# Layer 3 self-attention on one Trainium2 core: half of the penalties' products on GpSimd instead of VectorE

## The chip, the cores and the metric

One Trainium2 chip, one of its cores, one launch. The time is device microseconds of that core for the whole kernel, a twelve-part decoder (four layers of self-attention, cross-attention and feed-forward). Engines are named as the profile names them: PE is TensorE's matmul stream and PEld its weight loads, DVE is VectorE, ACT is ScalarE, POOL is GpSimd, SP is SyncE, which issues the loads.

## The reference

Tokens are x[16,128,256], seen as (2, 512, 256) or (4, 512, 256) by some layers and as 16 blocks of 128 here. The part that the change touches is layer 3's self-attention:

```python
g = sigmoid(x @ Wg + bg)
res = (1 - Z_I) * max(1 - Z_I - Z_J, 0) + Z_I * min(1 - Z_I + Z_J, 1)
penalties = res * clip(base ** (1 - g) + 2 - abs_ij, 1e-32, 1)
scores = q @ k.T / sqrt(16) + log(max(penalties, 1e-32))    # 16 heads of 16
ctx = softmax(scores) @ v
x = layernorm(x + ctx)
```

The kernel does not add the logarithm ahead of the exponential. It multiplies exp(scores) by the penalties, one 128x128 table per block, the same for all heads; the sum of each row comes out of the product with V, which has columns of ones.

## The kernel before, in words

`attention16` serves several attentions. `l3_attentions` calls it with two parts in one pipeline: 16 "own" blocks (the self-attention, with penalties) and then 16 "crossed" blocks (the cross-attention, without). A block is 128 tokens with 16 heads, handled in two halves of 8 heads; a half is one 128x1024 float32 tile. Its stages are spread over turns: `for n in TURNS` on each engine writes out by hand what that engine does in turn n, in order, and engines meet at counted semaphores (`since(engine, event, b)` waits until event has counted block b). Nothing else orders the work.

In turn n, of own blocks:
- PE (L2402): scores of block n, first half, interleaved with the transposed scores of block n-1, half 1 (`scores(n, 0)`, L2301 and L2306); `attend(n-2)` (L2336), half 1 and then half 0 of the probabilities `Pr` times V, each after `w_done[half]`; queries of block n+1; the transposes of a finished block (L2384); then `before_second(n)`, which waits for `mx_ready[0]`, and `scores(n, 1)`; after it the transposes of the output (L2343), the keys of n+1 (L2256), the transposes of the maxima (L2368) and the values of n+1 (L2267).
- ACT (L2506): the exponentials of block n-1, half 1 after `scores(n, 0)` and half 0 after `scores(n, 1)` (L2447, they count `e_done[half]`); between them copies out of PSUM, and the keys' placing (L2478).
- DVE (L2607): `maximum(n, 0)` (L2547); `spread(n-3)`, the moments of a row (L2595 to L2599); **`weigh(n-1, 1)`** (L2560); `maximum(n, 1)` (L2547); `scaled(n-3)` (L2605); `put_maxima(n)` (L2554); `weigh(n-1, 0)` (L2560); `normalise(n-2)` (L2579, L2584).
- POOL (L2227): `move_v(n)` (L2196); `root(n-3)` (L2221); `own_query(n+1)`, four instructions (L2210); `store(n-3)` (L2225), after `scaled(n-3)`; `own_residual(n-2)` (L2217), after `normalise(n-2)`.

`weigh(b, half)` multiplies the 128x1024 tile of probabilities in place by the penalties' 128x128 table, read again for each of the 8 heads:

```python
dve.tensor_tensor(Pr[b % 2][half][:].rearrange("p j c n -> p (j c) n"),
                  Pr[b % 2][half][:].rearrange("p j c n -> p (j c) n"),
                  part(b).penalty[:, b, :].unsqueeze(1).to_broadcast([P, NH * SLOTS16, P]),
                  ALU.mult).then_inc(w_done[half], 1)
```

Turn n = 1 is the first with a `weigh` (block 0) and turn 16 the last (block 15). Two buffers of `Pr` are used in turn (`b % 2`); the exponential of block b waits for `attend(b-2)`. Other lines that the prediction uses: L1878, a POOL product `tensor_tensor(k2, k2, table, mult)` of a 128x1024 tile in place with a 128-wide table, in another stage; L4400, L4503 and L4504, POOL and DVE operations on 128x512 tiles in the stage that makes the penalties. The stage after the attention asks for its first data at L3190 once the attention has ended.

Of the kernel before, what the change touches and what calls it, by code (L numbers as in the profile page):

```python
# [8 lines left out]
ALU = mybir.AluOpType  # L9
# [7 lines left out]
P = 128  # L17
# [19 lines left out]
NH = P // ROWS // 2  # L37
# [2022 lines left out]
def attention16(core, a, name, parts, after=()):  # L2060


    with Stage(core, name) as s:
        SCALE = float(DH) ** -0.5
        LIFT = 60.0
        SLOTS16 = KD * PAIR
# [23 lines left out]
        Pr = [[s.sb(f"Pr{w}_{i}", [P, NH, SLOTS16, P]) for i in range(2)] for w in range(2)]  # L2090
# [30 lines left out]
        e_done = [s.sem(f"e_done{i}") for i in range(2)]  # L2121
        w_done = [s.sem(f"w_done{i}") for i in range(2)]
# [13 lines left out]
        def live(b):  # L2136

            return 0 <= b < LAST

        def own(b):  # L2140

            return live(b) and part(b).own

        def crossed(b):

            return live(b) and not part(b).own

        def part(b):

            return parts[b // NB]  # L2150

        def block_of(b):

            return b % NB

        def since(eng, event, b):

            if b >= 0:
                eng.wait_ge(event, min(b, LAST - 1) + 1)
# [6 lines left out]
        @block.sync  # L2166
        def _(sp):
            for later in after:
                later.request(sp, a)

        @block.gpsimd
        def _(pool):
            pool.memset(mx[:], 0.0).then_inc(m_cleared, 1)
            if any(p.penalty is not None for p in parts):
                pool.memset(lift[:], LIFT).then_inc(lift_ready, 1)
            for t in V:
                pool.memset(t[:], 1.0).then_inc(v_cleared, 1)
            for p in parts:
                p.early.wait(pool)
                if p.moved:  # L2180
                    pool.wait_ge(biases_ready, 1)
            pool.wait_ge(v_cleared, len(V))

            def sum_q(b):
                since(pool, q_turned, b)
                since(pool, q_stored, b - 1)
                pool.tensor_tensor(q32[:], rq[0][:], rq[1][:], ALU.add).then_inc(q_summed, 1)

            def move_v(b):
                since(pool, o_ready, b - len(V))  # L2190
                out = V[b % len(V)][:, :, 0:DH]
                if part(b).values is not None:
                    ins = pool.tensor_copy(out, part(b).values[:, block_of(b), :].rearrange("p (h d) -> p h d", d=DH))
                else:
                    since(pool, v_copied, b)
                    ins = pool.tensor_tensor(out, v32[:].rearrange("p (h d) -> p h d", d=DH),  # L2196
                                             part(b).early.bvt[:].rearrange("p (h d) -> p h d", d=DH), ALU.add)
                ins.then_inc(v_stored, 1)

            def residual(b):  # L2200
                since(pool, r_ready, b - 1)
                since(pool, x_stored, b - NB)
                x = core.X[:, block_of(b), :]
                pool.tensor_tensor(xres[:], x, part(b).early.bot[:], ALU.add).then_inc(xres_ready, 1)

            def own_query(b):
                since(pool, q_copied, b)
                since(pool, t_ready[0], b - 4)
                for c in range(SLOTS16):
                    ins = pool.tensor_scalar(qx[b % 4][:, c, :], q32[:, c % KD, :], own_rows[:, c // KD:c // KD + 1],  # L2210
                                             bqm[:, c:c + 1], ALU.mult, ALU.add)
                ins.then_inc(q_stored, 1)

            def own_residual(b):
                since(pool, normal, b)
                since(pool, xn_ready, b - 1)
                pool.tensor_tensor(r[:], O[:], core.X[:, block_of(b), :], ALU.add).then_inc(r_ready, 1)  # L2217

            def root(b):
                since(pool, ve_ready, b)  # L2220
                pool.tensor_tensor(rstd[:], ve[:], core.mhalf[:], ALU.pow).then_inc(rstd_ready, 1)  # L2221

            def store(b):
                since(pool, xn_ready, b)
                pool.tensor_copy(core.X[:, block_of(b), :], xn[:]).then_inc(x_stored, 1)  # L2225

            for n in TURNS:  # L2227
                if crossed(n - 3):
                    residual(n - 3)
                if live(n):  # L2230
                    move_v(n)
                if own(n - 3):
                    root(n - 3)
                if own(n + 1):
                    own_query(n + 1)
                if own(n - 3):
                    store(n - 3)
                if crossed(n - 4):
                    root(n - 4)
                if rope and live(n + 1):  # L2240
                    sum_q(n + 1)
                if crossed(n - 4):
                    store(n - 4)
                if own(n - 2):
                    own_residual(n - 2)
# [285 lines left out]
        def _(dve):  # L2531
# [11 lines left out]
            def maximum(b, half):  # L2543
                since(dve, s_ready[half], b)
                since(dve, m_ready, b - 1)
                out = mx[:].rearrange("p t (e c) -> p e t c", c=DH)[:, NH * PAIR * half:NH * PAIR * (half + 1), :, 0]
                dve.tensor_reduce(out, pR[:].rearrange("p j (i t) n -> p (j i) t n", i=PAIR), AX.X, ALU.max  # L2547
                                  ).then_inc(mx_ready[half], 1)
# [9 lines left out]
            def weigh(b, half):  # L2558
                since(dve, e_done[half], b)
# [5 lines that stand above are left out]
            def rotate(b):  # L2565
                since(dve, q_ready, b)
                since(dve, q_summed, b - 1)
                for out, table in ((rq[0], early.cosT), (rq[2], early.sin_partner)):
                    for t in range(KD):
                        ins = dve.scalar_tensor_tensor(out=out[:, t, :], in0=pq[:, t, :], scalar=early.bqc[:, t:t + 1],  # L2570
                                                       in1=table[:], op0=ALU.add, op1=ALU.mult)
                ins.then_inc(q_placed, 1)
                dve.wait_ge(q_placed, b + 1)
                dve.stream_shuffle(out=rq[1][:].rearrange("p k n -> p (k n)"), in_=rq[2][:].rearrange("p k n -> p (k n)"),
                                   mask=partners()).then_inc(q_turned, 1)
# [17 lines left out]
            def spread(b):  # L2593
                dve.wait_ge(r_ready, b + 1)
                dve.bn_stats(stats[:], r[:]).then_inc(stats_ready, 1)  # L2595
                dve.wait_ge(stats_ready, b + 1)
                dve.bn_aggr(mv[:], stats[:]).then_inc(mv_ready, 1)
                dve.wait_ge(mv_ready, b + 1)
                dve.tensor_scalar(ve[:], mv[:, 1:2], LN_EPS, None, ALU.add).then_inc(ve_ready, 1)  # L2599
# [7 lines left out]
            for n in TURNS:  # L2607
                if live(n):
                    maximum(n, 0)
                if own(n - 3):  # L2610
                    spread(n - 3)
                if crossed(n - 4):
                    spread(n - 4)
                if own(n - 1):
                    weigh(n - 1, 1)
                if rope and live(n + 1):
                    rotate(n + 1)
                if live(n):
                    maximum(n, 1)
                if own(n - 3):  # L2620
                    scaled(n - 3)
                if crossed(n - 4):
                    scaled(n - 4)
                if live(n):
                    put_maxima(n)
                if own(n - 1):
                    weigh(n - 1, 0)
                if live(n - 2):
                    normalise(n - 2)
                if crossed(n - 3):  # L2630
                    residual(n - 3)
# [2061 lines left out]
```

## Time and profile before

| | us |
|---|---|
| median of 3 runs | 2595.38 (2594.41 to 2601.98) |
| the profiled execution | 2594.83 |
| its span | 2593.0 |
| PE busy | 2283.1 (88%) |
| DVE busy | 1314.9 (51%) |
| POOL busy | 709.2 (27%) |

The span is the time from the first to the last recorded instruction; the profiled execution's own time has 1.8 us around it. The rows below are quoted from the page and from answers of the trace: "x4" is a count of merged instructions, and "[0.64 <-PE a_pR L2301]" says that the engine sat idle for 0.64 us before the instruction and which work ended that. Where several instructions are merged, the duration is that of the whole group. Instructions on one engine can overlap a little at their ends, so the distance between two starts can be slightly less than a duration.

### The profile page before, as it was taken

How to read it: one execution, taken by the hardware profiler on the slowest of the kernel's cores; microseconds unless marked ns; L12 is line 12 of the kernel's file. 1: busy time of each engine (PE TensorE's matmuls, PEld its weight loads, DVE VectorE, ACT ScalarE, POOL GpSimd, SP SyncE). 2: the span in 40 equal slices, each digit the busy share in tenths (PEclk: the TensorE clock that was granted, in tenths of full speed). 3: DMA queues.
4: the chain of work that ended last, by engine and by line, in shares of the span. 5: the costliest groups of instructions: out<-in, count | busy, mean ns of one | idle time of the engine just before them, and what ended most of it. 6: DMA issues, size and time to landing. Idle time of an engine off the chain costs nothing. (4 is left out here: it accounts for less than half of the span.)

```text
span 2593.0 us, 48661 instructions
## 1 busy us (share of the span) xinstructions
PE 2283.1 (88%) x18360; PEld 1789.3 (69%) x18369; DVE 1314.9 (51%) x2768; ACT 906.4 (35%) x1591; POOL 709.2 (27%) x1096
## 2 busy tenths in 40 slices
PE   8869999787989899999979988976977989599992
PEld 4647777453567565899968866645865778399992
DVE  4466666598668421111157754553137887511114
ACT  2233333484356301111122224521225667122223
POOL 1722222235223100122212221211325633133332
PEclk9889999898989999999999998987988999799996
DMA  7500000100020100788710003012530000399994
GB/s 281 190 1 1 0 0 1 26 1 1 1 92 2 52 0 1 269 315 316 259 51 0 0 3 95 2 52 83 165 84 5 2 2 3 116 322 327 325 325 139
DMA packets 162728, 253.57 MB, mean 98 GB/s; under 512 B 17296, under 2 KB 123536, under 8 KB 162320
## 3 DMA queue, kind: packets, MB, share of 16 engines
q1 hardware_dynamic: 153360, 230.42, 25.8%
q0 software_dynamic: 9216, 21.06, 3.0%
q8 instruction: 103, 1.69, 0.3%
q14 instruction: 49, 0.40, 0.0%
HBM read 219.79 MB, written 31.13 MB: 97 GB/s over the span
## 5 line engine op out<-in xcount | busy, mean ns | idle before, releaser
L3516 PE MATMUL te_pU<-te_xsT,te_wu 128*128 128x128 f32 x1952 | 233.5, 276 | 1.5 <-DVE te_xsT L3609 1.5
L3516 PEld LDWEIGHTS te_pU<-te_xsT,te_wu 128*128 128x128 f32 x1952 | 231.1, 193 | 5.2 <-issue 2.1
L3537 PE MATMUL te_pY<-te_wd,te_hT 128*128 128x256 f32 x976 | 220.8, 379 | 0.0
L3537 PEld LDWEIGHTS te_pY<-te_wd,te_hT 128*128 128x128 f32 x976 | 180.7, 190 | 22.1
L1230 PE MATMUL x_pB<-early,x_xlT 128*128 128x384 f32 x376 | 133.4, 499 | 1.7 <-ACT x_xlT L1362 1.7
L3566 ACT ACTIVATE te_hT<-te_pU 128x512 f32<-128x512 f32 x78 | 46.6, 597 | 234.9 <-PE te_pU L3516 234.9
L2547 DVE TENSOR_REDUCE x_mx<-x_pR 128x8 f32<-128x1024 f32 x64 | 78.3, 1223 | 78.0 <-PE x_pR L2301 78.0
L3590 DVE COPY te_ys<-te_pY 128x256 f32<-128x256 f32 x61 | 25.9, 425 | 162.8 <-PE te_pY L3537 162.8
L3585 DVE TENSOR_TENSOR te_hT<-te_pU,te_sg 128x512 f32<-128x512 f32 x44 | 30.4, 692 | 147.5 <-ACT te_sg L3564 147.5
L3564 ACT ACTIVATE te_sg<-te_pG 128x512 f32<-128x512 f32 x44 | 26.3, 597 | 210.2 <-PE te_pG L3516 210.2
L1230 PEld LDWEIGHTS x_pB<-early,x_xlT 128*128 128x128 f32 x376 | 68.8, 193 | 43.1 <-issue 4.3
L2547 DVE TENSOR_REDUCE a_mx<-a_pR 128x8 f32<-128x1024 f32 x64 | 78.3, 1224 | 34.2 <-PE a_pR L2301 34.1
L2449 ACT ACTIVATE x_Pr<-x_pT 128x1024 f32<-128x1024 f32 x64 | 65.6, 1025 | 79.8 <-PE x_pT L2306 79.8
L3587 DVE COPY te_xsT<-te_pT 128x256 f32<-128x256 f32 x61 | 25.7, 421 | 130.6 <-PE te_pT L3510 130.6
L2301 PE MATMUL a_pR<-a_kx,a_qx 32*128 32x128 f32 x1024 | 74.6, 282 | 17.1 <-ACT a_kx L2478 6.3
L3478 POOL COPY te_home<-moe_home 128x1 uint32 (+1 forms) x61 | 11.1, 181 | 285.0 <-DVE te_ys L3590 285.0
L2301 PEld LDWEIGHTS a_pR<-a_kx,a_qx 32*128 32x128 f32 x1024 | 63.4, 186 | 33.1 <-issue 20.0
L3516 PE MATMUL te_pG<-te_xsT,te_wg 128*128 128x128 f32 x704 | 85.8, 275 | 0.0
L2301 PEld LDWEIGHTS x_pR<-x_kx,x_qx 32*128 32x128 f32 x1024 | 66.5, 196 | 25.0 <-issue 21.7
L2301 PE MATMUL x_pR<-x_kx,x_qx 32*128 32x128 f32 x1024 | 79.0, 294 | 4.3 <-DVE x_qx L2554 3.7
L3516 PEld LDWEIGHTS te_pG<-te_xsT,te_wg 128*128 128x128 f32 x704 | 82.1, 192 | 0.0
L3468 POOL DMA_INDIRECT te_xs<-xs_slots,te_token x65 | 64.8, 997 | 51.9 <-POOL te_token L3465 51.9
(669 smaller groups left out, 5627.1 us busy)
## 6 DMA issues: line engine op xcount, KB each, us to landing
te_wu<-in_L_ffn_w_upT SPq DMA_DIRECT2D x39, 1024.0 KB, 5.9
te_wd<-in_L_ffn_w_downT SPq DMA_DIRECT2D x39, 1024.0 KB, 5.8
te_wu<-in_L_ffn_up SPq DMA_DIRECT2D x22, 1024.0 KB, 4.9
te_wg<-in_L_ffn_gate SPq DMA_DIRECT2D x22, 1024.0 KB, 6.9
te_wd<-in_L_ffn_down SPq DMA_DIRECT2D x22, 1024.0 KB, 7.6
moe_first<-in_L_ffn_W SPq DMA_DIRECT2D x8, 1024.0 KB, 8.5
xs_slots<-zeros SPq DMA_DIRECT2D x1, 5120.0 KB, 15.6
ys_slots<-zeros SPq DMA_DIRECT2D x1, 5120.0 KB, 28.9
```

Of the source, the lines that this page charges most:

```text
L1230: ins = pe.matmul(to[:, n, 0:HALF], xlT[t][:, src + k, :], w[:, k, bass.ts(n, HALF)], start=(k == 0), stop=(k == KD - 1))
L2301: return pe.matmul(pR[:, j, c, :], qx[b % 4][g, c, :], kx[b % 4][g, c, :], start=mask is None, stop=mask is None or c == SLOTS16 - 1)
L2449: ins = act.activation(Pr[b % 2][half][:], pT[:], ACT.Exp, scale=SCALE)
L2547: dve.tensor_reduce(out, pR[:].rearrange("p j (i t) n -> p (j i) t n", i=PAIR), AX.X, ALU.max).then_inc(mx_ready[half], 1)
L3468: pool.indirect_dma_start(xs[u][:], None, core.XS, bass.IndirectOffsetOnAxis(token[u][:, 0:1], 0)).then_inc(x_loaded[u], 16)
L3516: ins = pe.matmul(out[g][:, m, :], w[:, k, bass.ts(PER * g + m, P)], xsT[:, k, :], start=(k == 0), stop=(k == KD - 1))
L3537: ins = pe.matmul(pY[u][:, 0, :], hT[:, k, :], wd[u][:, k, :], start=(k == 0), stop=(k == KH - 1))
L3564: act.activation(sg[g][:], pG[g][:], act_fn).then_inc(g_done, 1)
L3566: act.activation(hT[:, PER * g:PER * (g + 1), :], pU[g][:], act_fn).then_inc(h_done, 1)
L3585: dve.tensor_tensor(hT[:, PER * g:PER * (g + 1), :], pU[g][:], sg[g][:], ALU.mult).then_inc(h_done, 1)
L3587: dve.tensor_copy(xsT[:], pT[:, 0:KD, :]).then_inc(xT_stored, 1)
L3590: dve.tensor_copy(ys[u][:], pY[u][:, 0, :]).then_inc(y_used, 1)
```

## The change

`weigh(n-1, 1)` is taken out of DVE's order of turn n, where it stood between `spread` and `maximum(n, 1)`. POOL gets a `weigh` of its own, for half 1 alone, placed behind `store(n-3)` and ahead of `own_residual(n-2)`. The operands, the event waited for (`e_done[1]`) and the event counted (`w_done[1]`) are the same; half 0 stays on DVE.

```diff
--- before.py
+++ after.py
@@ -2216,6 +2216,12 @@
                 since(pool, xn_ready, b - 1)
                 pool.tensor_tensor(r[:], O[:], core.X[:, block_of(b), :], ALU.add).then_inc(r_ready, 1)
 
+            def weigh(b):
+                since(pool, e_done[1], b)
+                pr = Pr[b % 2][1][:].rearrange("p j c n -> p (j c) n")
+                pool.tensor_tensor(pr, pr, part(b).penalty[:, b, :].unsqueeze(1).to_broadcast([P, NH * SLOTS16, P]),
+                                   ALU.mult).then_inc(w_done[1], 1)
+
             def root(b):
                 since(pool, ve_ready, b)
                 pool.tensor_tensor(rstd[:], ve[:], core.mhalf[:], ALU.pow).then_inc(rstd_ready, 1)
@@ -2235,6 +2241,8 @@
                     own_query(n + 1)
                 if own(n - 3):
                     store(n - 3)
+                if own(n - 1):
+                    weigh(n - 1)
                 if crossed(n - 4):
                     root(n - 4)
                 if rope and live(n + 1):
@@ -2611,8 +2619,6 @@
                     spread(n - 3)
                 if crossed(n - 4):
                     spread(n - 4)
-                if own(n - 1):
-                    weigh(n - 1, 1)
                 if rope and live(n + 1):
                     rotate(n + 1)
                 if live(n):
```

## Rows read from the trace of the kernel before

**Rows 1.** Page: the span and the busy time of each engine.

```profile
span 2593.0 us, 48661 instructions
...
PE 2283.1 (88%) x18360; PEld 1789.3 (69%) x18369; DVE 1314.9 (51%) x2768; ACT 906.4 (35%) x1591; POOL 709.2 (27%) x1096
```

**Rows 2.** Windows, turns 3-13, 14-16: length, PE, PEld, DVE, ACT, POOL, PEclk.

```profile
2000.22:2089.32 89.10, 80.98 (x1365) 68.06 (x1366) 78.96 (x133) 57.53 (x110) 55.46 (x90) 1.00 0.01 2
2089.32:2111.22 21.90, 17.74 (x341) 14.44 (x342) 20.03 (x35) 14.76 (x27) 9.73 (x16) 1.00 0.01 1
```

**Rows 3.** Timeline of DVE, turns 8 and 9: start, duration, instruction, [idle before].

```profile
2040.72 1.23 DVE L2547 TENSOR_REDUCE a_mx<-a_pR 128x8 f32<-128x1024 f32 x1 [0.64 <-PE a_pR L2301]
...
2041.86 0.50 DVE L2605 TENSOR_SCALAR a_xn<-a_r,a_mv,a_rstd 128x256 f32<-128x256 f32 x1
...
2042.54 0.88 DVE L2554 SCALAR_TENSOR_TENSOR a_qx<-a_pX,place,a_qx 128x256 f32<-128x256 f32 x2 [0.17 <-PE a_pX L2368]
...
2043.33 1.22 DVE L2560 TENSOR_TENSOR a_Pr<-a_Pr,early 128x1024 f32<-128x1024 f32 x1
...
2045.09 1.22 DVE L2547 TENSOR_REDUCE a_mx<-a_pR 128x8 f32<-128x1024 f32 x1
...
2046.96 1.22 DVE L2560 TENSOR_TENSOR a_Pr<-a_Pr,early 128x1024 f32<-128x1024 f32 x1
...
2048.82 1.23 DVE L2547 TENSOR_REDUCE a_mx<-a_pR 128x8 f32<-128x1024 f32 x1 [0.64 <-PE a_pR L2301]
```

**Rows 4.** Timeline of PE in turns 8 and 9.

```profile
2043.79 0.34 PE L2301 MATMUL a_pR<-a_kx,a_qx 32*128 32x128 f32 x1 [0.42 <-ACT a_kx L2478]
...
2045.28 1.08 PE L2336 MATMUL a_pO<-a_Pr,a_V 128*32 128x128 f32 x32 [0.31 <-issue]
...
2047.28 0.38 PE L2384 MATMUL a_pk<-ident,a_xn 128*128 128x128 f32 x2
...
2047.60 0.37 PE L2301 MATMUL a_pR<-a_kx,a_qx 32*128 32x128 f32 x1
```

**Rows 5.** Timeline of POOL in turns 8 and 9.

```profile
2040.48 1.73 POOL L2210 TENSOR_SCALAR a_qx<-a_q,own_rows,a_bqm 128x128 f32<-128x128 f32 x4
...
2042.43 0.40 POOL L2225 COPY X<-a_xn 128x256 f32<-128x256 f32 x1 [0.21 <-DVE a_xn L2605]
...
2045.26 0.73 POOL L2217 TENSOR_TENSOR a_r<-a_O,X 128x256 f32<-128x256 f32 x1 [2.44 <-DVE a_O L2584]
...
2047.12 1.46 POOL L2221 TENSOR_TENSOR a_rstd<-a_ve,mhalf 128x1 f32<-128x1 f32 x1 [0.44 <-DVE a_ve L2599]
```

**Rows 6.** Timeline of DVE: second maxima of turns 3, 14, 15 and 17.

```profile
2000.22 1.23 DVE L2547 TENSOR_REDUCE a_mx<-a_pR 128x8 f32<-128x1024 f32 x1 [0.42 <-PE a_pR L2301]
...
2089.32 1.23 DVE L2547 TENSOR_REDUCE a_mx<-a_pR 128x8 f32<-128x1024 f32 x1 [0.64 <-PE a_pR L2301]
...
2096.70 1.22 DVE L2547 TENSOR_REDUCE a_mx<-a_pR 128x8 f32<-128x1024 f32 x1
...
2111.22 1.23 DVE L2547 TENSOR_REDUCE a_mx<-a_pR 128x8 f32<-128x1024 f32 x1 [0.83 <-PE a_pR L2301]
```

**Rows 7.** One line's instructions on POOL: products and roots, min/median/max ns.

```profile
L1878 POOL TENSOR_TENSOR a_turned<-a_turned,early x4: 2347/2794/2797, 597.8 to 637.4; 128x1024 f32<-128x1024 f32 x4
...
L2221 POOL TENSOR_TENSOR a_rstd<-a_ve,mhalf x32: 548/550/1491, 1998.7 to 2221.9; 128x1 f32<-128x1 f32 x32
```

**Rows 8.** Timeline of POOL and DVE where both work on 128x512 tiles.

```profile
1953.73 1.54 POOL L4400 TENSOR_TENSOR ao_high<-ao_oz,ao_zj 128x512 f32<-128x512 f32 x1 [2.79 <-ACT ao_oz L4456]
...
1953.68 0.69 DVE L4503 TENSOR_TENSOR ao_low<-ao_oz,ao_zj 128x512 f32<-128x512 f32 x1 [0.74 <-ACT ao_oz L4456]
...
1954.41 1.41 DVE L4504 SCALAR_TENSOR_TENSOR ao_low<-ao_low,ao_oz 128x512 f32<-128x512 f32 x1
```

**Rows 9.** Timeline of POOL and DVE beside POOL's 128x1024 products.

```profile
597.75 2.35 POOL L1878 TENSOR_TENSOR a_turned<-a_turned,early 128x1024 f32<-128x1024 f32 x1
...
605.59 2.80 POOL L1878 TENSOR_TENSOR a_turned<-a_turned,early 128x1024 f32<-128x1024 f32 x1
...
597.81 14.66 DVE L2009 SCALAR_TENSOR_TENSOR a_cv<-a_xi,early,a_cv 128x512 f32<-128x512 f32 x6 [2.90 <-ACT a_cv L1956]
```

**Rows 10.** Timeline of SP's queue after the attention.

```profile
2224.08 0.38 SPq L3190 DMA_DIRECT2D xs_slots<-X  x1
```

## The prediction

> **What bounds the kernel now.** I read the page's first part, then the windows over the stage, then the timelines of one turn engine by engine, and last the durations of single lines. The page says that PE is busy for 88% of the span and POOL for 27% [rows 1]. That is an average over many stages and says nothing of this one. In the turns that the change touches, the windows show PE busy 80.98 of 89.10 us, DVE 78.96, POOL 55.46 [rows 2]: PE and DVE are both near full, and the granted clock is 1.00, so TensorE has its full 2.4 GHz. One turn is the distance between two second maxima, (2089.32 - 2000.22)/11 = 8.10 us [rows 6].
>
> DVE in one turn [rows 3]: the second maxima at 2040.72 came 0.64 us after DVE had run out of work, because PE's scores were late. So the product that the change removes (2046.96, the half 1 product of block 8) stands ahead of a wait for PE, 0.64 us long. What opens PE's second scores at 2047.60 is PE's own row of work: `attend` at 2045.28, queries, then the transposes at 2047.28 with 0.38 us [rows 4]. The first maxima, which they also wait for, end at 2045.09 + 1.22 = 2046.31 [rows 3], 1.29 us early. PE's first scores wait 0.42 us for ACT's keys [rows 4], again not for DVE. So in turns 3 to 13 PE with ACT sets the pace, and DVE follows closely. In turns 14 and 15 it is DVE: no idle time stands before 2096.70, and that turn took 2096.70 - 2089.32 = 7.38 us [rows 6].
>
> **What is removed.** One DVE product per turn, 1.22 us, some 1.14 us from start to next start, 16 times. In turns 3 to 13 that only lengthens DVE's idle 0.64 us: worth nothing. Where DVE sets the pace it is worth at most 1.14 us per turn, if nothing else is late. It also ends a collision: POOL's root takes 1.46 us at 2047.12, beside this product [rows 5], and 0.55 us in the median of the stage [rows 7]. That is off the path, since POOL then idles 2.44 us ahead of L2217 [rows 5].
>
> **What is added.** One product on POOL per turn. L1878 is its near twin (in place, both inputs in SBUF, 128x1024, a repeated table): 2.35 us at the least and 2.80 at the most [rows 7]. I take 2.35, the instruction at 597.75 that began with DVE idle [rows 9]; 2.80 is the upper end, beside DVE work. POOL has room: 55.46 us busy in 11 turns is 5.04 per turn [rows 2], minus 0.91 for the root, plus 2.35, makes 6.5 of 8.10. The hole is exactly where the product is put, between the store's end at 2042.43 + 0.40 = 2042.83 and L2217 at 2045.26 [rows 5]. 2042.83 + 2.35 = 2045.18 is 0.10 us ahead of `attend` at 2045.28 [rows 4]. By durations alone the change would cost nothing.
>
> **The collision.** But DVE's other product, half 0 of the same block, starts at 2043.33 [rows 3], inside that interval, and both instructions read two tiles of SBUF. What then happens is shown elsewhere in the trace. L4504 on DVE takes 1.41 us when it starts at 1954.41, while POOL's L4400 runs from 1953.73 to 1955.27; the like operation before it, L4503, took 0.69 [rows 8]. It ended at 1955.82, 0.55 us after POOL's: it had waited for POOL, with only 0.69 - 0.55 = 0.14 us of its own done meanwhile. Six DVE operations of that size took 14.66 us, 2.44 each, beside POOL's products of 2.35 to 2.80 [rows 9]: about one DVE operation passed per POOL operation. The root's 1.46 us is the same with DVE first. So whoever starts first holds the other up, and here POOL starts first, by 2043.33 - 2042.83 = 0.50 us.
>
> The Trainium skill, "SBUF — State Buffer", section "Who interferes with whom", says the same of a VectorE instruction with two SBUF inputs against a GpSimd instruction that reads SBUF, and speaks of an exclusive lock held for the whole instruction. Taken to the letter (1.22 us after POOL's end in place of 1.08) it would add 0.14 us per turn, about 2 us in all; the rows show the 0.14 overlapped, and the sum goes by them.
>
> **The sum for one turn**, in us after the start of the second maxima (2040.72 is 0):
> - POOL's `own_query` ends later than now: POOL's L2217 and all behind it move with DVE's late normalise, the root gives back 0.91, and about 0.2 is left. The store then ends at 2.11 + 0.2 = 2.3.
> - POOL's product runs from 2.3 to 4.65. DVE's wants to start at 2.61 and is held; it ends at 4.65 + 1.22 - 0.14 = 5.73, instead of 3.83.
> - `attend` takes half 1 first, which is ready at 4.65, 0.1 late. Half 0 starts now at 2045.28 + 0.5 - 2040.72 = 5.06 and would start at about 5.8: 0.74 late. PE has no slack behind it (queries, transposes, second scores), so the turn grows by 0.74.
> - By DVE: from the product to the first maxima it is 2045.09 - 2043.33 = 1.76, so these end at 5.73 - 1.22 + 1.76 + 1.22 = 7.49; they are needed at 6.88 (2047.60). That gives 0.61, beside and not on top of the other.
>
> I take 0.7 us per turn. A turn of 8.8 us holds it steadily, as each delay is repeated and not piled up.
>
> **The stage.** Turns 3 to 13, 11 x 0.7 = 7.7 us. Turns 14 and 15, paced by DVE: the blocked product adds about 1.7 us and the removed one gives back 1.14, so 0.6 and 0.5. Turn 16: DVE is 1.64 late, the next second maxima have 0.83 of idle time before them [rows 6], so 0.8. Turns 1 and 2, while the pipeline fills, nothing: there POOL and DVE idle more than a product's length. Sum 9.6 us. Nothing later takes it up: the next stage asks for its rows only at 2224.08 [rows 10], after the attention, so the rest moves as a block. Against the profiled execution's 2594.83 us this is 2604.4; the median of the runs, 2595.38, stands 0.55 above that execution, within its scatter, and I keep 2604.4.
>
> **Rivals.** A measurement of this kernel can tell about 0.3%, 7.8 us, from no change. The forecast stands only just beyond that.
> - **Forecast, POOL first, +9.6 us**, 0.62. With the uncertain terms: if the product takes 2.80, +0.45 per turn and 14 turns, +6; if DVE is held shorter (a POOL instruction's last part free of reads; in rows 9, 0.69 + 2.35 = 3.04 was done in 2.8), 0.3 less per turn, -4. So +5.5 to +16.
> - **No hold-up that reaches the path, 0 us**, 2594.8, 0.17. Half 0 is ready at 3.83 now and needed at 5.06; if DVE's product is held for less than that 1.23 us, PE and the maxima take it up. For it: this slack, and POOL's hole, which fits to 0.1 us. Against it: rows 8 and 9 show the hold.
> - **DVE first**, slower, +17 us, 2612, 0.12. If POOL's store slips past 2.61, DVE's product runs first and POOL's ends at 3.83 + 2.0 = 5.8; `attend` takes half 1 first, and waits from 4.56 to 5.85, 1.3 per turn, 13 turns. Against it: the margin is 0.3 to 0.5 us, and the delay it makes gives POOL time to be early in the next turn.
> - **Faster**, the other side: if PE's pace in turns 14 to 16 follows DVE alone and the two products miss each other there and before, 3 x 1.14 = 3.4 us at most, 2591.4. It would need POOL's product to be over by 2.61, 0.3 us after it starts, or DVE to read past it, and would still be within 0.3%. More than that would need PE's wait of 0.42 us to be for DVE, and the row names ACT. 0.09 with unknown gains, 0.04 of them beyond 0.3%.
>
> The forecast's own spread crosses the bound of 7.8 us, so slower is 0.60, the same 0.36, faster 0.04. The range, 2596 to 2611, takes in both ends of the hold-up, most of the longer product, and leaves out the extreme cases on either side.
>
> **What would show it.** In the profile after: L2560 falls from 32 to 16 instructions and each shows about 3.1 us (from 2.61 to 5.73) instead of 1.22; POOL's product shows 2.35 us, right behind L2225; the root falls to 0.55; the second maxima are 8.8 us apart; PE is idle some 0.7 us inside `attend`, waiting for DVE. Wrong would be: L2560 still at 1.22 with turns of 8.1 (no hold-up); POOL's product at 3 us or more and `attend` late at its first half (DVE first); or turns longer than 9.2 us.

## The result and the profile after

| | before | after |
|---|---|---|
| median | 2594.89 us (4 runs) | 2633.09 us (2631.60 to 2635.69, 4 runs) |
| ratio | | 1.0144, 95% interval 1.0132 to 1.0157 |
| the profiled execution | 2594.83 us | 2635.69 us |

The change made the kernel 38 us slower. The direction was forecast; the size, +9.6 us, was four times too small, and the range ended at 2611. The page of the changed kernel begins so; DVE and POOL are busy about as long as before in all, beside [rows 1]:

```profile
span 2633.9 us, 48661 instructions
...
PE 2302.9 (87%) x18360; PEld 1804.8 (69%) x18369; DVE 1318.8 (50%) x2752; ACT 906.2 (34%) x1591; POOL 732.8 (28%) x1112
```

Windows over turns 3 to 13 and 14 to 16 of the changed kernel, the same turns as in [rows 2]. The columns are length, busy time (instructions) of PE, PEld, DVE, ACT and POOL, granted clock, DMA:

```profile
2007.87:2121.49 113.62, 88.08 (x1365) 74.20 (x1366) 82.89 (x122) 57.46 (x110) 70.84 (x101) 0.92 0.01 2
2121.49:2150.82 29.33, 20.70 (x341) 16.88 (x342) 22.57 (x34) 15.45 (x27) 14.22 (x18) 0.88 0.01 1
```

Turns 3 to 13 took 113.62 us instead of 89.10, turns 14 to 16 29.33 instead of 21.90. That is 32.0 of the 40.9 us by which the two spans differ. The granted clock fell from 1.00 to 0.92 and 0.88, which no row of before had announced. Another 0.8 us is in the first turns of the stage; 6.9 us had passed before the stage began and 1.2 us came behind it, in parts that the change does not touch.

The two products, summed up over the stage (count, then min/median/max ns), and then DVE around one turn, with the second maxima at 2059.25 and 2070.26. They answer to [rows 7] and [rows 3]:

```profile
L2222 POOL TENSOR_TENSOR a_Pr<-a_Pr,early x16: 2352/2358/2365, 1992.7 to 2142.5; 128x1024 f32<-128x1024 f32 x16
...
L2568 DVE TENSOR_TENSOR a_Pr<-a_Pr,early x16: 1576/2800/2814, 1994.5 to 2143.1; 128x1024 f32<-128x1024 f32 x16
```

```profile
2051.38 0.88 DVE L2562 SCALAR_TENSOR_TENSOR a_qx<-a_pX,place,a_qx 128x256 f32<-128x256 f32 x2 [0.28 <-PE a_pX L2376]
...
2052.17 2.81 DVE L2568 TENSOR_TENSOR a_Pr<-a_Pr,early 128x1024 f32<-128x1024 f32 x1
...
2055.18 0.42 DVE L2592 TENSOR_TENSOR a_O<-a_pO,a_R 128x256 f32<-128x256 f32 x1
...
2055.52 1.22 DVE L2555 TENSOR_REDUCE a_mx<-a_pR 128x8 f32<-128x1024 f32 x1
...
2059.25 1.23 DVE L2555 TENSOR_REDUCE a_mx<-a_pR 128x8 f32<-128x1024 f32 x1 [1.77 <-PE a_pR L2309]
...
2070.26 1.23 DVE L2555 TENSOR_REDUCE a_mx<-a_pR 128x8 f32<-128x1024 f32 x1 [3.11 <-PE a_pR L2309]
```

POOL's product takes 2.36 us every time, as its near twin did at its shortest (2.35). DVE's takes 2.80 us instead of 1.22: issued at 2052.17, it ends at 2054.98. POOL in the same turn, the answer to [rows 5]:

```profile
2051.17 0.40 POOL L2231 COPY X<-a_xn 128x256 f32<-128x256 f32 x1 [0.74 <-DVE a_xn L2613]
...
2051.53 2.36 POOL L2222 TENSOR_TENSOR a_Pr<-a_Pr,early 128x1024 f32<-128x1024 f32 x1
...
2055.68 0.73 POOL L2217 TENSOR_TENSOR a_r<-a_O,X 128x256 f32<-128x256 f32 x1 [1.79 <-DVE a_O L2592]
...
2057.55 0.55 POOL L2227 TENSOR_TENSOR a_rstd<-a_ve,mhalf 128x1 f32<-128x1 f32 x1 [0.46 <-DVE a_ve L2607]
```

POOL's product ends at 2053.89 and DVE's 1.09 us later, where the prediction had 1.08. The root is at 0.55 us. So both products and the root behave as forecast; only the start of POOL's product is 0.3 us earlier, which makes the hold-up shorter. The Trainium skill, "SBUF — State Buffer", section "Who interferes with whom", says that the instruction that comes second is blocked until the first has finished; the trace agrees, except that some 0.13 us of the 1.22 is done meanwhile.

What was not forecast is on PE. Its timeline, the attend and the queries of two turns, the answer to [rows 4]:

```profile
2055.70 1.08 PE L2344 MATMUL a_pO<-a_Pr,a_V 128*32 128x128 f32 x32 [1.90 <-DVE a_O L2592]
...
2056.72 1.16 PE L2264 MATMUL a_pq<-XT,early 128*128 128x128 f32 x8
...
2065.39 1.93 PE L2344 MATMUL a_pO<-a_Pr,a_V 128*32 128x128 f32 x32 [1.90 <-DVE a_O L2592]
...
2067.25 1.64 PE L2264 MATMUL a_pq<-XT,early 128*128 128x128 f32 x8
```

`attend` starts at 2055.70, after the end of DVE's `normalise` at 2055.18 + 0.42 = 2055.60, not after the product with which it works. Its wait is 1.90 us in both turns, where [rows 4] show 0.31. In the second of them the same 32 matmuls take 1.93 us instead of 1.08 and the queries 1.64 instead of 1.16. Windows of 10 us around these and two further turns have the granted clock as the third number from the end of a row:

```profile
2050.00:2060.00 10.00, 7.68 (x129) 6.50 (x129) 7.85 (x12) 5.54 (x11) 6.73 (x11) 1.00 0.01 2
2060.00:2070.00 10.00, 7.68 (x119) 6.44 (x117) 6.78 (x11) 4.51 (x10) 5.40 (x8) 0.83 0.01 2
2090.00:2100.00 10.00, 7.67 (x102) 6.43 (x104) 7.17 (x11) 4.78 (x10) 5.24 (x8) 0.83 0.01 2
2100.00:2110.00 10.00, 7.68 (x144) 6.50 (x141) 7.54 (x11) 5.34 (x11) 6.74 (x10) 1.00 0.01 2
```

The turn ending at 2059.25 took 9.69 us and the one ending at 2070.26 11.01. In turns 3 to 13 there are six of 9.68 or 9.69 us and five of 11.00 to 11.22.

### The profile page after: what moved, and what is told of

It reads as the page before. It is cut to its first block and busy times, and to the rows that moved or that the text cites. A ratio compares the mean times of both kernels' runs of the same rounds, so it can differ in the third digit from the quotient of the medians.

```text
span 2633.9 us, 48661 instructions
## 1 busy us (share of the span) xinstructions
PE 2302.9 (87%) x18360; PEld 1804.8 (69%) x18369; DVE 1318.8 (50%) x2752; ACT 906.2 (34%) x1591; POOL 732.8 (28%) x1112
```

## Theories

Theory A: three things in a row. POOL's product, placed in POOL's hole, holds up DVE's product of the other half. DVE's `normalise` stands behind that product, and `attend(b)` on PE begins with a wait for `normalise(b-1)`, so the whole delay reaches PE. And PE's wait of 1.90 us costs granted clock in about every second turn. Its rivals: B, that 2.36 us of POOL per turn is too much or too late wherever it stands; that the long turns come from the order of the waits and not from the clock; and that the changed program is slower elsewhere too. The expectations below were written before each run.

## The experiments

**DVE's order.** In the changed kernel, `normalise(n-2)` goes ahead of `weigh(n-1, 0)`:

```diff
-                if own(n - 1):
-                    weigh(n - 1, 0)
                 if live(n - 2):
                     normalise(n - 2)
+                if own(n - 1):
+                    weigh(n - 1, 0)
```

> The changed kernel with normalise(n-2) ahead of weigh(n-1, 0) on DVE. Theory A (attend waits for normalise, which stands behind DVE's held product, and PE's wait of 1.90 us also costs granted clock): the held product stays (2.8 us beside POOL's 2.36) but attend's first half no longer waits for it, only its second half does; PE's longest wait falls from 1.9 us to under 1 us, turns fall from 9.69/11.1 us to about 8.8 us, and the kernel to about 2606 us (the 0.7 us per turn of the prediction). Theory B (POOL's product is itself too late for attend, or something outside the order of these two costs the time): turns stay above 9.5 us and the time above 2625 us.

Measured 2600.97 us (2599.76 to 2609.78, 10 runs), ratio to before 1.0025 (1.0011 to 1.0039). DVE, PE and POOL in one turn:

```profile
2053.37 0.42 DVE L2592 TENSOR_TENSOR a_O<-a_pO,a_R 128x256 f32<-128x256 f32 x1
...
2053.71 2.18 DVE L2568 TENSOR_TENSOR a_Pr<-a_Pr,early 128x1024 f32<-128x1024 f32 x1
...
2059.05 1.23 DVE L2555 TENSOR_REDUCE a_mx<-a_pR 128x8 f32<-128x1024 f32 x1 [1.29 <-PE a_pR L2309]
...
2054.96 0.65 PE L2344 MATMUL a_pO<-a_Pr,a_V 128*32 128x128 f32 x16 [0.24 <-POOL a_Pr L2222]
...
2055.95 0.64 PE L2344 MATMUL a_pO<-a_Pr,a_V 128*32 128x128 f32 x16 [0.35 <-DVE a_Pr L2568]
...
2052.44 2.37 POOL L2222 TENSOR_TENSOR a_Pr<-a_Pr,early 128x1024 f32<-128x1024 f32 x1
```

The hold-up is still there: DVE's product takes 2.18 us beside POOL's 2.37. Exchanging `normalise` and the product on DVE nevertheless took back most of the loss. `attend` now falls into two groups of 16 matmuls, the first 0.24 us late for POOL's product and the second 0.35 us late for DVE's, and turns 3 to 13 take 94.35/11 = 8.58 us at a clock of 1.00. This is the mechanism as the prediction had drawn it, in a kernel with another order. Theory A's 2606 us was 5 us too much.

**POOL's place.** In the changed kernel, POOL's product goes from behind `store(n-3)` to ahead of `root(n-3)`; DVE's order is the changed kernel's own:

```diff
                 if live(n):
                     move_v(n)
+                if own(n - 1):
+                    weigh(n - 1)
                 if own(n - 3):
                     root(n - 3)
...
-                if own(n - 1):
-                    weigh(n - 1)
```

> The changed kernel with POOL's product moved ahead of root(n-3), behind move_v(n), so that it runs beside DVE's maxima and moments and not beside DVE's product. Theory A (all of the loss comes from the overlap of the two products): DVE's product is back at 1.22 us, turns 3 to 13 at 8.1 us, turns 14 to 16 up to 1 us shorter each, and the kernel at 2591 to 2596 us. Theory B (POOL is too slow or late for this work wherever it stands): root, own_query and store are 2.36 us later, the second maxima's followers wait, and turns are 8.5 us or longer, the kernel above 2600 us.

Measured 2599.19 us (2595.52 to 2606.73, 10 runs), ratio 1.0020 (1.0005 to 1.0034). DVE's product, the second maxima ahead of and behind it, and POOL:

```profile
2046.39 1.23 DVE L2555 TENSOR_REDUCE a_mx<-a_pR 128x8 f32<-128x1024 f32 x1 [1.77 <-PE a_pR L2309]
...
2049.00 1.28 DVE L2568 TENSOR_TENSOR a_Pr<-a_Pr,early 128x1024 f32<-128x1024 f32 x1
...
2054.55 1.23 DVE L2555 TENSOR_REDUCE a_mx<-a_pR 128x8 f32<-128x1024 f32 x1 [1.77 <-PE a_pR L2309]
...
2044.21 2.37 POOL L2222 TENSOR_TENSOR a_Pr<-a_Pr,early 128x1024 f32<-128x1024 f32 x1
...
2046.53 0.56 POOL L2227 TENSOR_TENSOR a_rstd<-a_ve,mhalf 128x1 f32<-128x1 f32 x1
...
2047.07 1.79 POOL L2210 TENSOR_SCALAR a_qx<-a_q,own_rows,a_bqm 128x128 f32<-128x128 f32 x4
```

The same 2.37 us of work on POOL, at a time when DVE runs maxima and moments and no product, and DVE's product is at 1.28 us and the turn at 8.16. B falls: the amount of work on POOL costs 0.06 us a turn here, its place in the changed kernel 1.6 us and more. The kernel is still not the 2591 to 2596 us expected. Its profiled run was 2595.52, with one turn of 8.88 us at a reduced clock (the mean of turns 14 to 16 is 0.93); the ten runs scatter over 11 us. The four at 2604.5 us or more have a mean granted clock of 0.940 or 0.941, the six others 0.945 or 0.946, so the rest of the loss goes with the clock; why it falls in some runs and not in others was not settled.

**Work for PE in its wait.** In the changed kernel the query projection is issued twice; the first result is overwritten by the second:

```diff
+            def refresh(b):
+                since(pe, xT_stored, b - NB)
+                since(pe, q_copied, b - 1)
+                since(pe, v_copied, b - 1)
+                project(pq, (part(b).early.wq,), core.XT, b)
...
                 if live(n - 2):
+                    if own(n + 1):
+                        refresh(n + 1)
                     attend(n - 2)
```

> The changed kernel with the query projection of the next block issued twice, the first time ahead of attend, into the same PSUM region and with the same waits, so that PE has 8 more matmuls (about 1.1 us) to do while it waits for DVE. Theory A (long turns of 11.0 to 11.2 us come from a lower granted clock that follows PE's 1.90 us wait): PE waits 0.8 us, the clock stays at 1.00 through the stage, every turn of 3 to 13 is 9.7 us, and although PE does more work the kernel is 7 to 12 us faster than the changed one, about 2623 us. Theory B (the long turns come from the order of waits, for instance POOL late every second or third turn): the long turns stay and the kernel is at 2633 us or slower.

Measured 2628.91 us (2620.24 to 2630.65, 4 runs), ratio 1.0120 (1.0093 to 1.0146). Windows of turns 3 to 13 and 14 to 16:

```profile
2008.56:2115.09 106.53, 93.11 (x1453) 78.77 (x1454) 82.87 (x122) 57.46 (x110) 70.87 (x101) 1.00 0.01 2
2115.09:2143.76 28.67, 20.47 (x341) 16.96 (x342) 22.10 (x34) 15.44 (x27) 14.22 (x18) 0.88 0.01 2
```

With 88 more matmuls, turns 3 to 13 take 106.53 us instead of 113.62, all of them 9.68 or 9.69 us, at a clock of 1.00. From turn 15 on no own block follows and there is no filler. The last `attend` with one and the first without, and the window from the second maxima ahead of the latter to the next ones:

```profile
2111.54 1.08 PE L2350 MATMUL a_pO<-a_Pr,a_V 128*32 128x128 f32 x32 [0.81 <-issue]
...
2121.23 1.08 PE L2350 MATMUL a_pO<-a_Pr,a_V 128*32 128x128 f32 x32 [1.90 <-DVE a_O L2600]
```

```profile
2115.09:2124.80 9.71, 7.39 (x117) 6.05 (x117) 7.52 (x11) 5.83 (x11) 5.56 (x8) 0.88 0.01 3
```

The wait is 1.90 us again and the clock falls in that same window, in the same execution. So the long turns are the clock's, and the clock follows what PE does in its wait. The gain expected in the median, 7 to 12 us, did not show: 4 us against the first runs of the changed kernel, none against its later ones (below). The evidence here is the turns, 7.1 us shorter in a profile, not the medians.

**The other half.** In the kernel before, half 0's product goes to POOL behind `store(n-3)`, and half 1's stays on DVE:

```diff
+            def weigh(b):
+                since(pool, e_done[0], b)
+                pr = Pr[b % 2][0][:].rearrange("p j c n -> p (j c) n")
...
-                if own(n - 1):
-                    weigh(n - 1, 0)
                 if live(n - 2):
                     normalise(n - 2)
```

> The kernel before with the other half moved: half 0's product on POOL behind store(n-3), half 1's left on DVE. The work moved is the same size; what differs is that the DVE instruction that attend's start hangs on (normalise) loses a product ahead of it, and that no DVE product runs beside POOL's. Theory A: POOL's product takes 2.36 us from 2.1 us after the second maxima and ends at 4.5, attend needs half 0 half a microsecond after its start; attend can start 0.2 to 0.3 us sooner, turns are 7.8 to 8.1 us, turns 14 to 16 up to 1 us shorter, and the kernel is at 2587 to 2596 us. Theory B (2.36 us of POOL per turn costs as such): slower than before by 5 us or more, as for half 1.

Measured 2590.68 us (2589.11 to 2599.68, 10 runs), ratio 0.9987 (0.9974 to 0.9999). DVE's `normalise` and product, PE's `attend` and POOL's product:

```profile
2041.66 0.43 DVE L2592 TENSOR_TENSOR a_O<-a_pO,a_R 128x256 f32<-128x256 f32 x1
...
2044.93 1.22 DVE L2568 TENSOR_TENSOR a_Pr<-a_Pr,early 128x1024 f32<-128x1024 f32 x1
...
2042.94 1.08 PE L2344 MATMUL a_pO<-a_Pr,a_V 128*32 128x128 f32 x32
...
2040.94 2.35 POOL L2222 TENSOR_TENSOR a_Pr<-a_Pr,early 128x1024 f32<-128x1024 f32 x1
```

POOL does as much work as in the changed kernel, and the kernel is 42 us faster than that one (38 us against its later runs, below). `normalise` is over at 2042.09, 0.85 us ahead of `attend`, which has no idle time before it. Turns 4 to 13 take 7.71 us.

**The changed kernel again**, with no edit:

> The changed kernel itself once more, beside new runs of the kernel before. Theory A: the stage of the change is about 32 us longer than before (287 against 255 us), in some turns 11.0 us and in the others 9.7; the 7 us that the first profile shows ahead of this stage (of which 4 us fall in layer 1's cross-attention, at a granted clock of 0.64 against 0.80 in its first 33 us) come and go from run to run, so the median is between 2627 and 2634 us. Theory B (the changed program is also slower elsewhere): the same 7 us stand in the same places.

Measured 2628.31 us (2627.00 to 2637.77, 4 runs), ratio 1.0129 (1.0112 to 1.0146). Windows of turns 3 to 13 and of the whole stage, which was 254.86 us before:

```profile
2008.98:2125.49 116.51, 91.08 (x1365) 76.59 (x1366) 82.81 (x121) 57.65 (x110) 70.85 (x100) 0.90 0.01 2
1977.24:2267.37 290.13, 239.11 (x3872) 201.14 (x3872) 204.05 (x356) 162.92 (x304) 137.63 (x213) 0.94 0.01 3
```

The stage took 290.13 us (287.59 in the first profile), 35.3 more than before. Both profiled runs stood at the upper end of their series (2635.69 and 2637.77), and both were 7 to 8 us late ahead of the stage, with 4 us of that in layer 1's cross-attention. The filler kernel's profile was 6.5 us late there too, those of the other kernels between 3 us early and 1 us late; the three other runs of this series lie at 2627.0 to 2629.1. So the stage makes up about 33 us. What the first series had above that goes with a lower mean granted clock, 0.937 to 0.941 against 0.942 and 0.943 in those three runs. The kernel before shows such a loss too: 9 of its 44 runs beside the experiments took 2601.6 to 2603.2 us, at 0.942 instead of 0.946 or 0.947. So a loss of 7 to 9 us comes without the change as well; whether the changed kernel meets it more often is not shown.

**PE's order.** In the changed kernel, the queries of block n+1 go ahead of `attend(n-2)`:

```diff
+                if own(n + 1):
+                    queries(n + 1)
                 if live(n - 2):
                     attend(n - 2)
-                if own(n + 1) or rope and live(n + 1):
+                if rope and live(n + 1):
                     queries(n + 1)
```

> The changed kernel with the queries of block n+1 issued ahead of attend(n-2) on PE, so that PE has useful work of 1.0 us in the wait for DVE. Theory A (attend's wait for normalise, which stands behind the held product, is the whole loss): the wait falls from 1.90 to 0.9 us, the clock stays at 1.00, turns are 8.7 us, and the kernel at about 2605 us. Theory B (it is DVE and POOL that have too much work, PE's order does not matter): turns stay at 9.7 us, and the kernel above 2620 us.

Measured 2611.83 us (2608.89 to 2612.98, 4 runs), ratio 1.0064 (1.0048 to 1.0081). PE's `attend`, and then the windows of turns 3 to 13 and 14 to 16:

```profile
2051.79 1.08 PE L2344 MATMUL a_pO<-a_Pr,a_V 128*32 128x128 f32 x32 [0.94 <-issue]
```

```profile
2000.98:2098.81 97.83, 82.64 (x1365) 68.39 (x1366) 85.90 (x122) 56.48 (x110) 71.15 (x101) 1.00 0.01 2
2098.81:2127.13 28.32, 20.49 (x341) 17.24 (x342) 21.86 (x34) 15.27 (x27) 14.91 (x19) 0.88 0.01 2
```

The wait is 0.94 us, turns 3 to 13 are 8.9 us each (not 8.7: POOL's product starts later, and DVE's takes 2.95 us) at a clock of 1.00, and 21 us of the 38 are gone, or 16 of the 34 by the runs of the changed kernel taken beside these, without touching DVE or POOL. In turns 14 to 16, whose `attend` has no queries left to fill the wait, the clock is 0.88 and they take nearly as long as in the changed kernel (28.32 against 29.33 us); that is why it is 2611.8 and not 2605.

**The same exchange in the kernel before.** `normalise(n-2)` ahead of `weigh(n-1, 0)`, the edit of the first experiment, with both products on DVE:

> The kernel before with normalise(n-2) ahead of weigh(n-1, 0) on DVE and nothing on POOL. Theory A (already before the change attend was started by DVE's normalise, and the half 0 product stood ahead of that on the path): turns fall from 8.10 to 7.7 us as in the run with half 0 on POOL, attend shows no idle time before it, and the kernel is 4 to 5 us faster, about 2589 us. Theory B (PE and ACT set the pace in those turns, as the prediction had it, and the gain of the run with half 0 on POOL came from DVE having less work): turns stay at 8.1 us and the time within 1 us of before.

Measured 2591.10 us (2589.01 to 2594.20, 10 runs), ratio 0.9985 (0.9976 to 0.9995). DVE, PE, and the windows of turns 3 to 13 and 14 to 16:

```profile
2055.23 0.42 DVE L2584 TENSOR_TENSOR a_O<-a_pO,a_R 128x256 f32<-128x256 f32 x1
...
2055.57 1.22 DVE L2560 TENSOR_TENSOR a_Pr<-a_Pr,early 128x1024 f32<-128x1024 f32 x1
...
2056.50 1.08 PE L2336 MATMUL a_pO<-a_Pr,a_V 128*32 128x128 f32 x32
```

```profile
1998.33:2083.18 84.85, 80.36 (x1365) 67.86 (x1366) 78.44 (x132) 56.23 (x110) 65.07 (x89) 1.00 0.01 3
2083.18:2104.79 21.61, 17.81 (x341) 14.27 (x342) 19.98 (x36) 14.70 (x27) 12.72 (x17) 1.00 0.01 2
```

`attend` has no idle time before it, turns are 7.71 us and the whole kernel 0.15% faster than before. DVE does as much as before; only the order changed. So in the kernel before, `normalise` did start `attend`. Its row has "0.31 <-issue" [rows 4], but DVE's `normalise` had ended 0.11 us before it:

```profile
2044.75 0.42 DVE L2584 TENSOR_TENSOR a_O<-a_pO,a_R 128x256 f32<-128x256 f32 x1
```

In the changed kernel, whose row names DVE, the same distance is 2055.70 - 2055.60 = 0.10 us. So the 0.11 us is what passes between the two when `attend` does wait for `normalise`, and not slack.

**Both cures in the changed kernel**: POOL's product ahead of `root(n-3)`, and `normalise` first:

> The changed kernel with both cures: POOL's product ahead of root(n-3), where no DVE product runs, and normalise(n-2) ahead of weigh(n-1, 0) on DVE. Theory A: no product is held (POOL 2.37, DVE 1.22 to 1.3 us), turns of 7.7 us paced by PE and ACT's keys, turns 14 to 16 at 7.2 us or less, the stage at 250 us or less and the kernel at 2588 to 2591 us, the same as with the product of half 0 on POOL. Theory B (POOL's work delays q or xn once the turn is shorter): turns of 7.9 us or longer.

Measured 2590.92 us (10 runs, nine of them 2589.48 to 2596.23 and one of 4750.78 that nothing here explains), ratio 0.9984 (0.9972 to 0.9995). Windows of turns 3 to 13 and 14 to 16:

```profile
2000.69:2085.57 84.88, 80.31 (x1365) 67.81 (x1366) 65.80 (x121) 56.30 (x110) 81.27 (x100) 1.00 0.01 3
2085.57:2106.40 20.83, 17.60 (x341) 14.26 (x342) 17.89 (x33) 14.71 (x27) 16.34 (x20) 1.00 0.01 2
```

Turns of 7.72 us, and 0.8 us less than the kernel above in turns 14 to 16. This is the changed kernel's idea with nothing in its way. DVE is relieved by 12.6 us in turns 3 to 13 (65.80 against 78.44), and that brings nothing there: PE's wait of 0.42 us for ACT's keys and PE's own work set the 7.7 us.

The three kernels at 2590.7 to 2591.1 us cannot be told apart. Each is better than both kernels of the study, than the one before by 0.13 to 0.16%; the smallest edit among them leaves everything on DVE.

## Why the prediction was wrong

- **What bounds the kernel: half right.** PE and ACT set part of the pace, but the turn of 8.10 us was also held by DVE's `normalise`, by 0.39 us (8.10 - 7.71). The prediction read `attend`'s start at 2045.28 as PE arriving there. It did not follow the chain that ends in `attend`: the first maxima's slack of 1.29 us was worked out, the slack of `normalise` was not. Between its end and `attend` lay 2045.28 - 2045.17 = 0.11 us, no more than when `attend` waits for it: the slack was nil.
- **What is removed: right.** Worth nothing in turns 3 to 13, and the root fell to 0.55 us.
- **What is added: right.** 2.36 us against 2.35, and POOL had room; ahead of the root it makes turns of 8.16 against 8.10.
- **The collision: right.** POOL first, DVE held, end 1.09 us behind POOL's. The shown duration is 2.80 and not 3.1 us, since POOL's product started at 2051.53 - 2049.56 = 1.97, not 2.3, after the second maxima.
- **The sum for one turn: the step that failed.** It said "`attend` takes half 1 first, which is ready at 4.65, 0.1 late. Half 0 starts now at ... 5.06 and would start at about 5.8: 0.74 late." But `attend` does not start its first half before `normalise` of the block before, `since(pe, normal, b - 1)` in its second line of code. The same sum speaks of "DVE's late normalise", but carries it to POOL alone; its own 5.73 instead of 3.83, carried to `attend`, would have been 1.9 us a turn. PE's wait grew by 1.90 - 0.31 = 1.59 us, and the turn from 8.10 to 9.69. With the order in which the step holds (`normalise` first), the same hold-up made the turn 8.58 and not 7.71: 0.87, and 0.48 above before.
- **The clock: missing.** The prediction left TensorE at 1.00 and did not ask what PE's longer wait would do. Five turns of 3 to 13 were 1.3 to 1.5 us longer for it, 7.1 us together. 11 x 1.59 = 17.5, plus 7.1, is the 24.5 us of these turns. In turns 14 to 16 both together made 7.4 us where 1.9 was forecast. The sign "turns longer than 9.2 us", which the prediction had named for being wrong, is what came.
- **The rivals.** "DVE first" had a size nearer the truth (+17) by a mechanism that never occurred; "no hold-up" and "faster" fell to the first row of L2568. The range took every uncertain duration into account and no uncertain edge of the dependency graph.
- **Nothing later takes it up: right.** The difference was the same to 1.2 us from the stage's end to the kernel's.

## What to carry to other kernels

When an instruction on one engine will be delayed, list every wait at the head of its followers in the code, not only the data that the follower reads: here the wait for `normalise`, right behind the held product, had no slack and turned a hold-up of 1.6 us into 1.6 us per turn. A distance of 0.1 us between the end of one instruction and the start of another that waits for it is no slack, whatever the profile names as the releaser. A hole on an engine is free only if nothing that runs beside it is held up by what is put there; the same 2.36 us cost 38 us in one place of POOL's order and 5 us in another, and with the other half of the probabilities the kernel became faster. And before moving work to another engine, look whether two neighbours in the order of the busy one can be exchanged.

## What the runs showed of the hardware that was not expected

- After waits of 1.90 us, one in each turn of 9.7 us, PE fell from 2.4 to 1.2 GHz for part of about every second turn: the mean granted clock of windows of 10 us went from 1.00 to 0.83, and the same 32 matmuls took 1.93 instead of 1.08 us. With 1.0 us of matmuls put into the wait (0.81 and 0.94 us of idle time left), the clock stayed at 1.00 in all eleven turns, in two different kernels, and was at 0.88 once they were gone. In the second profile of the changed kernel one turn was 12.57 us, so the loss differs from run to run.
- A POOL instruction can be the one held, as the root of [rows 5] showed: in the three kernels with `normalise` ahead of DVE's product, POOL's 128x256 addition (0.73 us in [rows 5]) met that product and took 1.64 to 1.71 us.
- An idle time marked "issue" ahead of an instruction with several waits was in truth another engine's work, which had ended 0.1 us before. The changed kernel's profile names DVE at the same place, with 1.90 us.
